# A ternary 3x3 convolution after group norm: work ahead of image 0 reordered, Newton step and edge rows on ScalarE

## The chip, the cores and the metric

The kernel runs on one core of a Trainium2 chip. The metric is device time in microseconds for one execution. The core has TensorE (PE: matmul, PEld: its weight loads), VectorE (DVE), ScalarE (ACT), GpSimd (POOL) and SyncE (SP, which only issues DMAs here).

## What is computed

The input x has 32 images of 128 channels and 56 x 56 pixels, float32. Each image is normed in 32 groups of 4 channels, convolved 3 x 3 with weights made ternary, and added to itself.

```python
def _quantize(weight, Wp, Wn):
    max_val = jnp.max(jnp.abs(weight))
    safe_max = jnp.where(max_val > 0, max_val, jnp.ones_like(max_val))
    w_norm = jnp.where(max_val > 0, weight / safe_max, weight)
    delta = THRESHOLD * jnp.max(jnp.abs(w_norm))
    tern = jnp.where(w_norm > delta, 1.0, jnp.where(w_norm < -delta, -1.0, 0.0)).astype(weight.dtype)
    wq = jnp.where(tern > 0, Wp[0] * tern, jnp.where(tern < 0, Wn[0] * tern, tern))
    return wq
wq = _quantize(weight, Wp, Wn)
out = jax.lax.conv_general_dilated(x, wq, window_strides=(1, 1), padding=((1, 1), (1, 1)), ...)
return out + bias[None, :, None, None]
def _gn(v, G=32, eps=1e-05):
    ...
    return ((g - m) / jnp.sqrt(s + eps)).reshape(v.shape)
x = x + _L0_conv_ref(_gn(x), L0_conv_weight, L0_conv_bias, L0_conv_Wp, L0_conv_Wn)
```

THRESHOLD is 0.05, and m and s are mean and variance of a group in one image. In the inputs Wp and Wn are both 1.

## The kernel before

**Planes.** Channels lie on the 128 partitions. The three kernel rows are replaced by four products on half as many rows: from the 28 even and 28 odd rows of an image VectorE makes plane C (even + odd - 2 mean, `make_c`), D (odd - even, `make_d`) and A (differences of neighbouring odd rows, `make_a`), and GpSimd makes B (differences of even rows, `difference_b`, once the low part of C of the same image is there). One row of A and one of B lie at the image's edge, and ScalarE fills them (`edges`). The arrays `plane[0..3]` are shared by all images, one after another.

**Parts.** Each plane is scaled by the image's `norm_scale` and split into two float16 parts: ScalarE writes the high part (`make_hi`), VectorE the low one (`make_lo`, which needs the high). TensorE multiplies per product 4 banks of 6 matmuls (`multiply`), C and A into the even rows' PSUM banks, D and B into the odd rows'. A accumulates upon C and B upon D, so ScalarE copies the finished C and D products out in between (`copy_c`, `copy_d`), and VectorE combines each pair into y (`output_rows`, four passes, `y e` and `y o`). GpSimd issues a DMA that adds x, and SP stores y.

**Statistics.** ScalarE sums an image (`sum_x`), TensorE averages over the group with a one-column matmul, ScalarE takes the mean (`take_mean`), sums squares (`sum_squares`), TensorE averages, and VectorE makes the negated variance (`variance`). Then ScalarE takes a square root (`root`), VectorE its reciprocal (`first_rstd`), and VectorE refines it with one Newton step in two instructions (`newton_factor`, `scale_of_x`), which gives `norm_scale`.

**Order.** Every engine's order is written by hand in its `emit(prev, now, nxt, far)`, one slot for each image `now`: products and outputs of `now`, planes and factor of `nxt`, sum and mean of `far`. Engines meet only by semaphores, and a waiting instruction holds up everything behind it on its engine. There are a slot ahead of image 0 (`first_slot`, only `nxt`), the slot of image 0 (`second_slot`), then the ordinary ones, of which 24 lie in a loop. In an ordinary slot VectorE does: low D, variance, low A, planes C and D of the next image, reciprocal, Newton, low B, plane A, low C, four outputs. ScalarE does: high A, high B, copy C, root, sum, copy D, high C, mean, high D, squares, edges.

**Ahead of image 0.** ScalarE's queue issues the DMAs for wp, wn, the weights and the bias, and SP's issues those of images 0 to 3 in halves. VectorE finds the largest weight, makes the ternary weights (`w_pos`), and TensorE turns and combines them into four sets (`turn_weights`), which VectorE casts (`turned_weights`). TensorE then does 11 matmuls on constants (`warm_up`). `half_hi_ready` and `half_lo_ready` let the first product start upon half a plane. A second pass over everything follows only if Wp and Wn differ, which they don't here.

## Time and profile before

| | us |
|---|---|
| median of 3 executions | 574.85 (574.74 to 574.89) |
| profiled execution | 575.64 |
| its span, first to last instruction | 574.0 |
| VectorE busy | 542.9 (95%) |
| TensorE busy | 534.1 (93%) |
| ScalarE busy | 504.4 (88%) |
| GpSimd busy | 166.2 (29%) |
| mean granted TensorE clock | 0.989 of full |

Busy shares are of the span. Matmuls overlap, so TensorE's share counts time with at least one in flight. Times below are us from the span's start. The clock 1.00 is 2.4 GHz and 0.50 is 1.2 GHz.

### The profile page before, as it was taken

Reading aid. Unit: us, or ns where it says so; the run is one execution under the profiler, and the core shown is the slowest. Engines: PE = TensorE matmul, PEld = TensorE weight load, DVE = VectorE, ACT = ScalarE, POOL = GpSimd, SP = SyncE. Lnnn points to the kernel's source line nnn. Section 1 sums busy time; section 2 is a strip of 40 time slices with the busy share of each in tenths; the row PEclk is TensorE's granted clock in tenths of the full one; section 3 lists DMA queues with packets and bytes.
Section 4 is the critical chain, followed back from the end, with each engine's and each line's share of the span. In section 5 each row is a group of like instructions: output and inputs, shape, how many; then the busy total and the mean of one; then the engine's idle time right before and its main releaser. Section 6 shows DMA issues by size and latency. Waiting matters only on the chain.

```text
span 574.0 us, 9367 instructions
## 1 busy us (share of the span) xinstructions
PE 534.1 (93%) x3238; PEld 320.1 (56%) x3238; DVE 542.9 (95%) x506; ACT 504.4 (88%) x485; POOL 166.2 (29%) x107
## 2 busy tenths in 40 slices
PE   0597999999999999999999999999999999999994
PEld 0453555555555555555555555565555555555552
DVE  1986999999999999999999999999999999999994
ACT  3588999999999999999999999999999999999850
POOL 2203312333332223333222333332233333212330
PEclk9997999999999999999999999999999999999998
DMA  8433999999999999999999999999999999998767
GB/s 297 192 113 87 257 280 271 301 288 248 316 263 299 311 297 259 314 302 286 273 272 293 294 288 293 303 294 272 288 310 274 286 295 308 274 282 200 160 181 271
DMA packets 28104, 153.43 MB, mean 267 GB/s; under 512 B 3504, under 2 KB 3504, under 8 KB 28080
## 3 DMA queue, kind: packets, MB, share of 16 engines
q1 hardware_dynamic: 18576, 102.77, 47.1%
q0 software_dynamic: 8928, 49.78, 44.9%
q10 hardware_dynamic: 576, 0.59, 0.3%
q8 instruction: 12, 0.20, 0.1%
q14 instruction: 12, 0.10, 0.0%
HBM read 101.75 MB, written 51.38 MB: 267 GB/s over the span
## 4 chain that ended last, share of the span: by engine, by line
DVE 68%; issue 24%; PE 4%; DMA 2%; DVEq 1%; ACT 1%; ACTq 0%
DVE parts L581 25%; DVE y L600 18%; DVE plane L541 10%; DVE plane L547 10%; DMA y<-in_L_conv_weight_dram 2%; PE even_rows L732 2%; DVE newton L570 2%; PE odd_rows L732 1%; DVEq L157 1%; DVE plane L553 1%; DVE neg_var L559 1%; ACT parts L386 1%; DVE rstd L565 0%; PE even_rows L697 0%; DVE parts L587 0%
## 5 line engine op out<-in xcount | busy, mean ns | idle before, releaser
L732 PE MATMUL odd_rows<-parts,w_lhsT 128*128 128x385 f16 (+1 forms) x1536 | 266.8, 330 | 8.6 <-DVE parts L581 7.5
L732 PE MATMUL even_rows<-parts,w_lhsT 128*128 128x385 f16 (+1 forms) x1536 | 267.6, 331 | 3.7 <-DVE parts L587 2.9
L581 DVE SCALAR_TENSOR_TENSOR parts<-plane,norm_scale,parts 128x1568 f16<-128x1568 f32 x127 | 233.4, 1842 | 4.3 <-ACT parts L386 4.3
L324 POOL TENSOR_TENSOR plane<-x 128x1512 f32<-128x1512 f32 x32 | 109.2, 3413 | 384.1 <-DVE parts L581 366.9
L732 PEld LDWEIGHTS even_rows<-parts,w_lhsT 128*128 128x128 f16 x1536 | 150.0, 98 | 111.9 <-issue 8.7
L732 PEld LDWEIGHTS odd_rows<-parts,w_lhsT 128*128 128x128 f16 x1536 | 148.1, 100 | 108.2 <-DVE parts L581 9.4
L386 ACT ACTIVATE parts<-plane,norm_scale 128x1568 f16<-128x1568 f32 x127 | 199.8, 1597 | 9.8 <-ACT plane L426 5.2
L432 ACT ACTIVATE junk<-x,negmean 128x3136 f16<-128x3136 f32 x32 | 92.9, 2904 | 0.0
L392 ACT ACTIVATE junk<-x 128x3136 f16<-128x3136 f32 x31 | 86.9, 2804 | 0.0
L600 DVE SCALAR_TENSOR_TENSOR y<-even_rows,out_scale,d_sb 128x784 f32<-128x784 f32 x62 | 61.0, 1025 | 0.0
L600 DVE SCALAR_TENSOR_TENSOR y<-odd_rows,out_scale,c_sb 128x784 f32<-128x784 f32 x62 | 60.9, 1023 | 0.0
L541 DVE SCALAR_TENSOR_TENSOR plane<-x,neg2mean 128x1568 f32<-128x1568 f32 x32 | 59.0, 1844 | 0.0
L547 DVE TENSOR_TENSOR plane<-x 128x1568 f32<-128x1568 f32 x32 | 57.4, 1794 | 0.0
L377 ACT ACTIVATE d_sb<-odd_rows,bias_sb,out_scale 128x1568 f32<-128x1568 f32 x32 | 52.6, 1645 | 5.3 <-PE odd_rows L732 5.3
L337 POOL DMA_DIRECT2D y<-in_x_dram x62 | 54.4, 891 | 3.1 <-DVE y L600 0.5
L553 DVE TENSOR_TENSOR plane<-x 128x1512 f32<-128x1512 f32 x32 | 55.2, 1726 | 0.0
L371 ACT ACTIVATE c_sb<-even_rows,bias_sb,out_scale 128x1568 f32<-128x1568 f32 x32 | 52.5, 1641 | 1.7 <-PE even_rows L732 1.7
L417 ACT ACTIVATE neg2mean<-odd_rows 128x1 f32<-128x1 f32 x32 | 5.4, 170 | 26.5 <-PE odd_rows L718 21.9
L688 PE MATMUL odd_rows<-ident,w_absmax 128*128 128x128 f32 x1 | 0.4, 446 | 14.1 <-DVE w_absmax L503 14.1
L718 PEld LDWEIGHTS odd_rows<-sums,group_mean 128*128 128x128 f32 x62 | 10.9, 190 | 4.1 <-issue 1.8
L723 PEld LDWEIGHTS odd_rows<-sums,group_mean 128*128 128x128 f32 x64 | 11.6, 195 | 2.8 <-DVE parts L581 0.8
L503 DVE TENSOR_REDUCE w_absmax<-y 128x1 f32<-128x1152 f32 x1 | 1.4, 1353 | 11.6 <-DMA y<-in_L_conv_weight_dram 11.6
(65 smaller groups left out, 127.2 us busy)
## 6 DMA issues: line engine op xcount, KB each, us to landing
x<-in_x_dram SPq DMA_DIRECT2D x64, 784.0 KB, 11.7
out_dram<-y SPq DMA_DIRECT2D x63, 784.0 KB, 5.7
y<-in_x_dram POOLq DMA_DIRECT2D x62, 784.0 KB, 11.8
out_dram<-y SPq DMA_DIRECT2D x2, 392.0 KB, 6.2
y<-in_L_conv_weight_dram ACTq DMA_DIRECT2D x1, 576.0 KB, 10.7
wp_sb<-in_L_conv_Wp_dram ACTq DMA_DIRECT2D x1, 0.5 KB, 6.3
wn_sb<-in_L_conv_Wn_dram ACTq DMA_DIRECT2D x1, 0.5 KB, 7.9
bias_sb<-in_L_conv_bias_dram ACTq DMA_DIRECT2D x1, 0.5 KB, 12.2
```

The lines of the kernel that those rows point to most:

```text
L324: nc.gpsimd.tensor_tensor(plane[B][:, 0:PAIRS - 1, :], even[:, 0:PAIRS - 1, :], even[:, 1:, :], ALU.subtract).then_inc(plane_ready[B], 1)
L337: pool.dma_start(y, of, accum_op=ALU.add).then_inc(residual_added[img.buf][h], 16)
L377: nc.scalar.activation(d_sb[:], product_ps(ODD), ACT.Identity, bias=(no_bias if p else bias_sb)[:, 0:1], scale=out_scale[:, p, 1:2]).then_ ...
L386: nc.scalar.activation(part(img, j, HI), plane[j][:], ACT.Copy, scale=norm_scale[:, b_slice(img)]).then_inc(hi_ready[j], 1)
L392: nc.scalar.activation(junk[:], x_sb[img.buf][:].rearrange("p h w -> p (h w)"), ACT.Copy, accum_out=sums[:, img.buf, 1:2]).then_inc(sum_re ...
L432: nc.scalar.activation(junk[:], x_sb[img.buf][:].rearrange("p h w -> p (h w)"), ACT.Square, bias=negmean[:, b_slice(img)], accum_out=sums[ ...
L541: nc.vector.scalar_tensor_tensor(plane[C][:], xs[:, 0:H:2, :], neg2mean[:, b_slice(img)], xs[:, 1:H:2, :], ALU.add, ALU.add).then_inc(plan ...
L547: nc.vector.tensor_tensor(plane[D][:], xs[:, 1:H:2, :], xs[:, 0:H:2, :], ALU.subtract).then_inc(plane_ready[D], 1)
L553: nc.vector.tensor_tensor(plane[A][:, 1:, :], odd[:, 1:, :], odd[:, 0:PAIRS - 1, :], ALU.subtract).then_inc(plane_ready[A], 1)
L581: nc.vector.scalar_tensor_tensor(part(img, j, LO), plane[j][:], norm_scale[:, b_slice(img)], part(img, j, HI), ALU.mult, ALU.subtract).the ...
L600: nc.vector.scalar_tensor_tensor(rows_of(y_sb[img.buf], h, odd), product_ps(odd, 2 * h, 2 * h + 2), out_scale[:, p, 0:1], other[:, 2 * h:2 ...
L732: ins = nc.tensor.matmul(product_ps(odd, b, b + 1)[:, 0, :, to:to + n], w_lhsT[:, prod, kw, :], part(img, prod, which)[:, b * BANK_ROWS:(b ...
```

## The change

It does four things.

1. **Newton step on ScalarE.** VectorE keeps the reciprocal. The rest, in two instructions there, becomes three on ScalarE (square, times negated variance plus 3, times the first value), each waiting for the one before. In an ordinary slot they stand after the sum and ahead of `copy_d`.
2. **Edge rows in one instruction.** The four planes become one array `planes`, so that both edge rows can be reached with one stride.
3. **Ahead of image 0.** The weights' DMA is first on ScalarE's queue; SP waits for it before it loads image 1. VectorE makes plane D between the largest weight and the ternary weights, and the output scales move to slot 0. TensorE sums the variance ahead of turning the weights, its warm-up has 6 matmuls, and the mean of image 1 follows it. ScalarE sums image 1 ahead of the first high parts. The turned A and B weights are cast after the first low parts, on which C no longer waits.
4. **Slots 0 and 1.** In slot 0 VectorE makes planes A and B of image 0, ScalarE takes mean and squares of image 1 first, and TensorE sums its variance between two banks of D. Plane A of image 1 moves from slot 0 to slot 1.

For a second pass the weights are loaded again.

```diff
-WARM_UP = 11
+WARM_UP = 6
...
-        plane = [sb(f"plane{j}", [P, PAIRS, W]) for j in range(4)]
+        planes = sb("planes", [P, 4, PAIRS, W])
+        plane = [planes[:, j] for j in range(4)]
...
@@ SP: emit
                             if img.buf != nxt.buf or img is nxt:
+                                if p == 0 and img is far:
+                                    sp.wait_ge(w_loaded, 16)
                                 load(img, 0, first=img is nxt)
...
@@ GpSimd: emit
-                    if nxt:
-                        difference_b(nxt, after_c=now)
+                    if now and nxt:
+                        difference_b(nxt)
...
@@ ScalarE
+            act.dma_start(w_raw, weight.rearrange("o i h w -> o (i h w)")).then_inc(w_loaded, 16)
             act.dma_start(wp_sb[:], wp.rearrange("(a b) -> a b", a=1).broadcast_to([P, 1])).then_inc(scalars_loaded, 16)
...
-                    xs, bias = x_sb[img.buf], negmean[:, b_slice(img)]
-                    nc.scalar.activation(plane[A][:, 0, :], xs[:, 1, :], ACT.Identity, bias=bias)
-                    nc.scalar.activation(plane[B][:, PAIRS - 1, :], xs[:, H - 2, :], ACT.Identity,
-                                         bias=bias).then_inc(edges_ready, 1)
+                    first, last = A * PAIRS, B * PAIRS + PAIRS - 1
+                    rows = planes[:].rearrange("p j r w -> p (j r) w")[:, first:last + 1:last - first, :]
+                    nc.scalar.activation(rows, x_sb[img.buf][:, 1:H - 1:H - 3, :], ACT.Identity,
+                                         bias=negmean[:, b_slice(img)]).then_inc(edges_ready, 1)
...
+                def scale_of_x(img):
+
+                    b = b_slice(img)
+                    act.wait_ge(rstd_ready, img.count(plus=1))
+                    nc.scalar.activation(rstd_sq[:, b], rstd0[:, b], ACT.Copy, scale=rstd0[:, b]).then_inc(rstd_sq_ready, 1)
+                    act.wait_ge(rstd_sq_ready, img.count(plus=1))
+                    nc.scalar.activation(newton[:, b], rstd_sq[:, b], ACT.Identity, bias=three[:, 0:1],
+                                         scale=neg_var[:, b]).then_inc(newton_ready, 1)
+                    act.wait_ge(newton_ready, img.count(plus=1))
+                    nc.scalar.activation(norm_scale[:, b], newton[:, b], ACT.Copy,
+                                         scale=rstd0[:, b]).then_inc(scale_of_x_ready, 1)
...
@@ VectorE
-                def newton_factor(img):
-                    b = b_slice(img)
-                    dve.wait_ge(rstd_ready, img.count(plus=1))
-                    nc.vector.tensor_scalar(newton[:, b], rstd0[:, b], rstd0[:, b], neg_var[:, b],
-                                            ALU.mult, ALU.mult).then_inc(newton_ready, 1)
...
+                def make_first_b(img):
+                    plane_free(img, B)
+                    even = x_sb[img.buf][:, 0:H:2, :]
+                    nc.vector.tensor_tensor(plane[B][:, 0:PAIRS - 1, :], even[:, 0:PAIRS - 1, :], even[:, 1:, :],
+                                            ALU.subtract).then_inc(plane_ready[B], 1)
...
@@ TensorE: emit
                         sum_first_mean(nxt)
-                        turn_weights()
                         pe.wait_ge(negmean_ready, nxt.count(plus=1))
                         sum_var(nxt, start=True)
+                        turn_weights()
                         warm_up()
+                        pe.wait_ge(var_ready, nxt.count(plus=1))
+                        sum_mean(far, start=True)
                     if second_slot:
-                        pe.wait_ge(w_ready, 4 * p + 4)
+                        pe.wait_ge(w_ready, 4 * p + 2)
```

How the orders stand now, at three places. First ScalarE in an ordinary slot, from the high parts of A and B to the means of the image after next. `parts` is the high part, `junk,sums<-x` the sum, `std` the root. Before:

```order
L386 ACTIVATE parts<-plane,norm_scale 128x1568 x2
L371 ACTIVATE c_sb<-even_rows,bias_sb,out_scale 128x1568
L438 ACTIVATE std<-neg_var 128x1
L392 ACTIVATE junk,sums<-x 128x3136
L377 ACTIVATE d_sb<-odd_rows,bias_sb,out_scale 128x1568
L386 ACTIVATE parts<-plane,norm_scale 128x1568
L417 ACTIVATE neg2mean<-odd_rows 128x1
```

and in the change:

```order
L392 ACTIVATE parts<-planes,norm_scale 128x1568 x2
L377 ACTIVATE c_sb<-even_rows,bias_sb,out_scale 128x1568
L444 ACTIVATE std<-neg_var 128x1
L398 ACTIVATE junk,sums<-x 128x3136
L451 ACTIVATE rstd_sq<-rstd 128x1
L453 ACTIVATE newton<-rstd_sq,three,neg_var 128x1
L456 ACTIVATE norm_scale<-newton,rstd 128x1
L383 ACTIVATE d_sb<-odd_rows,bias_sb,out_scale 128x1568
L392 ACTIVATE parts<-planes,norm_scale 128x1568
L423 ACTIVATE neg2mean<-odd_rows 128x1
```

The three Newton instructions have come in between the sum and the copy of D. The first waits for VectorE's reciprocal, and the copy of D and the high part of C stand behind them.

Second, VectorE in the same slot, from the low part of A to the low part of C of the next image (`parts` is the low part, `plane<-x` are planes C, D and A). Before:

```order
L581 SCALAR_TENSOR_TENSOR parts<-plane,norm_scale,parts 128x1568
L541 SCALAR_TENSOR_TENSOR plane<-x,neg2mean 128x1568
L547 TENSOR_TENSOR plane<-x 128x1568
L565 RECIPROCAL rstd<-std 128x1
L570 TENSOR_SCALAR newton<-rstd,neg_var 128x1
L576 TENSOR_SCALAR norm_scale<-newton,rstd 128x1
L581 SCALAR_TENSOR_TENSOR parts<-plane,norm_scale,parts 128x1568
L553 TENSOR_TENSOR plane<-x 128x1512
L581 SCALAR_TENSOR_TENSOR parts<-plane,norm_scale,parts 128x1568
```

In the change:

```order
L616 SCALAR_TENSOR_TENSOR parts<-planes,norm_scale,parts 128x1568
L582 SCALAR_TENSOR_TENSOR planes<-x,neg2mean 128x1568
L588 TENSOR_TENSOR planes<-x 128x1568
L612 RECIPROCAL rstd<-std 128x1
L616 SCALAR_TENSOR_TENSOR parts<-planes,norm_scale,parts 128x1568
L594 TENSOR_TENSOR planes<-x 128x1512
L616 SCALAR_TENSOR_TENSOR parts<-planes,norm_scale,parts 128x1568
```

The two Newton instructions behind the reciprocal are gone, and nothing else of this slot has moved on VectorE.

Third, VectorE ahead of image 0 and at the start of slot 0, from the ternary weights on. Before:

```order
L523 SCALAR_TENSOR_TENSOR w_pos<-y,w_consts,w_neg 128x1152
L541 SCALAR_TENSOR_TENSOR plane<-x,neg2mean 128x1568
L531 CAST w_lhsT<-even_rows 128x384 x2
L559 TENSOR_SCALAR neg_var<-odd_rows 128x1
L531 CAST w_lhsT<-even_rows 128x384
L565 RECIPROCAL rstd<-std 128x1
L570 TENSOR_SCALAR newton<-rstd,neg_var 128x1
L576 TENSOR_SCALAR norm_scale<-newton,rstd 128x1
L531 CAST w_lhsT<-odd_rows 128x384
L547 TENSOR_TENSOR plane<-x 128x1568
L587 SCALAR_TENSOR_TENSOR parts<-plane,norm_scale,parts 128x784 x2
L553 TENSOR_TENSOR plane<-x 128x1512
```

In the change:

```order
L551 SCALAR_TENSOR_TENSOR w_pos<-y,w_consts,w_neg 128x1152
L606 TENSOR_SCALAR neg_var<-odd_rows 128x1
L582 SCALAR_TENSOR_TENSOR planes<-x,neg2mean 128x1568
L612 RECIPROCAL rstd<-std 128x1
L572 CAST w_lhsT<-even_rows 128x384 x2
L622 SCALAR_TENSOR_TENSOR parts<-planes,norm_scale,parts 128x784 x2
L572 CAST w_lhsT<-odd_rows 128x384 x2
L616 SCALAR_TENSOR_TENSOR parts<-planes,norm_scale,parts 128x1568
L594 TENSOR_TENSOR planes<-x 128x1512
```

The variance has moved ahead of plane C, plane D to a place before the ternary weights (not in the piece), and the third and fourth casts of weights behind the two half passes of the low part.

## Rows read from the trace of the kernel before

**Rows 1.** The page's part 4, chain that ended last: share of the span by engine.
```profile
DVE 68%; issue 24%; PE 4%; DMA 2%; DVEq 1%; ACT 1%; ACTq 0%
```

**Rows 2.** Timeline, VectorE, one steady period: start us, duration us, engine, line, operation.
```profile
313.94 1.84 DVE L581 SCALAR_TENSOR_TENSOR parts<-plane,norm_scale,parts 128x1568 f16<-128x1568 f32 x1
...
326.53 0.16 DVE L565 RECIPROCAL rstd<-std 128x1 f32<-128x1 f32 x1
326.72 0.27 DVE L570 TENSOR_SCALAR newton<-rstd,neg_var 128x1 f32<-128x1 f32 x1
...
327.16 1.84 DVE L581 SCALAR_TENSOR_TENSOR parts<-plane,norm_scale,parts 128x1568 f16<-128x1568 f32 x1
...
330.56 1.84 DVE L581 SCALAR_TENSOR_TENSOR parts<-plane,norm_scale,parts 128x1568 f16<-128x1568 f32 x1
```

**Rows 3.** Timeline, ScalarE, the same period; in brackets idle time and releaser.
```profile
317.56 0.33 ACT L425 ACTIVATE plane<-x,negmean 128x56 f32<-128x56 f32 x1
317.80 0.33 ACT L426 ACTIVATE plane<-x,negmean 128x56 f32<-128x56 f32 x1
318.30 3.10 ACT L386 ACTIVATE parts<-plane,norm_scale 128x1568 f16<-128x1568 f32 x2 [0.17 <-ACT plane L426]
...
325.73 1.64 ACT L377 ACTIVATE d_sb<-odd_rows,bias_sb,out_scale 128x1568 f32<-128x1568 f32 x1
327.28 1.60 ACT L386 ACTIVATE parts<-plane,norm_scale 128x1568 f16<-128x1568 f32 x1
329.67 0.17 ACT L417 ACTIVATE neg2mean<-odd_rows 128x1 f32<-128x1 f32 x1 [0.80 <-PE odd_rows L718]
```

**Rows 4.** Groups by line and form, ScalarE: busy us, mean ns | idle before.
```profile
L371 ACT ACTIVATE c_sb<-even_rows,bias_sb,out_scale 128x1568 f32<-128x1568 f32 x32 | 52.5, 1641 | 1.7 <-PE even_rows L732 1.7
L425 ACT ACTIVATE plane<-x,negmean 128x56 f32<-128x56 f32 x32 | 10.6, 332 | 0.0
```

**Rows 5.** Timeline, ScalarE, mean and squares of image 0.
```profile
15.32 0.17 ACT L418 ACTIVATE negmean<-odd_rows 128x1 f32<-128x1 f32 x1
15.52 2.91 ACT L432 ACTIVATE junk<-x,negmean 128x3136 f16<-128x3136 f32 x1
```

**Rows 6.** Timeline, VectorE, first output passes of image 1 and of image 30.
```profile
66.47 1.97 DVE L600 SCALAR_TENSOR_TENSOR y<-even_rows,out_scale,d_sb 128x784 f32<-128x784 f32 x2
...
548.33 1.97 DVE L600 SCALAR_TENSOR_TENSOR y<-even_rows,out_scale,d_sb 128x784 f32<-128x784 f32 x2
```

**Rows 7.** The page's part 6, the weights' DMA: KB, us from issue to landing.
```profile
y<-in_L_conv_weight_dram ACTq DMA_DIRECT2D x1, 576.0 KB, 10.7
```

**Rows 8.** Timeline, all engines, ahead of and in slot 0.
```profile
7.20 1.51 ACT L400 ACTIVATE junk<-x 128x1568 f16<-128x1568 f32 x1 [2.39 <-DMA x<-in_x_dram]
...
9.07 1.51 ACT L403 ACTIVATE junk<-x 128x1568 f16<-128x1568 f32 x1 [0.27 <-ACT junk L400]
...
14.61 0.29 DVE L512 TENSOR_REDUCE w_max<-odd_rows 128x1 f32<-128x128 f32 x1 [0.27 <-PE odd_rows L688]
...
17.60 1.42 DVE L523 SCALAR_TENSOR_TENSOR w_pos<-y,w_consts,w_neg 128x1152 f16<-128x1152 f32 x1
...
25.91 1.97 DVE L587 SCALAR_TENSOR_TENSOR parts<-plane,norm_scale,parts 128x784 f16<-128x784 f32 x2
...
27.08 4.15 PE L732 MATMUL even_rows<-parts,w_lhsT 128*128 128x392 f16 x24 [2.88 <-DVE parts L587]
...
47.86 1.97 DVE L600 SCALAR_TENSOR_TENSOR y<-even_rows,out_scale,d_sb 128x784 f32<-128x784 f32 x2
```

**Rows 9.** Windows: us, busy of PE, PEld, DVE, ACT, POOL (count), PEclk, DMA, GB/s.
```profile
24.20:27.00 2.80, 0.00 (x0) 0.00 (x0) 2.80 (x3) 2.00 (x3) 0.14 (x1) 1.00 0.00 0
...
46.20:47.20 1.00, 0.98 (x4) 0.55 (x5) 1.00 (x1) 1.00 (x1) 0.00 (x0) 0.59 0.00 0
...
52.00:53.00 1.00, 1.00 (x5) 0.46 (x4) 1.00 (x1) 1.00 (x2) 1.00 (x2) 0.50 0.59 63
...
299.09:531.72 232.63, 229.24 (x1402) 137.88 (x1401) 231.62 (x212) 219.27 (x211) 72.19 (x42) 1.00 1.00 285
```

More of the change, by code:

```diff
@@ L788, in emit @@
                         pe.wait_ge(d_ready, now.count(plus=1))
[L789 to L791 removed]
+                        if far and not second_slot:
                             sum_mean(far, start=False)
```

170 lines of the change are left out of this document (93 added, 77 removed).

## Prediction

> **What bounds the kernel now.** I read the page's chain of waits first. It lies on VectorE for 68% of the span, and another 24% is "issue", time between instructions in which nothing is waited for [rows 1]. So I went to the timeline of VectorE in the middle of the run. From one low-part pass over plane C (313.94) to the next (330.56) there are 16.62 us, and VectorE starts each instruction as the one before runs out [rows 2]. The first output pass of image 1 starts at 66.47 and that of image 30 at 548.33, so 29 periods last 481.86 us, 16.616 us each [rows 6]. VectorE is the bound of every slot. ScalarE has one real gap in its slot, 0.80 us ahead of the mean, and a gap of 0.17 us where it waits for its own edge rows [rows 3]. It is nearly as full, and this is what matters here, since the change takes work from the fullest engine and gives it to the next.
>
> Ahead of image 0 it is different. Slot 0 starts its products at 27.08 and its outputs at 47.86 [rows 8]. From there to 66.47 are 18.61 us, 2.0 more than a period, with TensorE at half its clock between them [rows 9].
>
> **The steady slots, what goes.** VectorE loses the two Newton instructions. The reciprocal starts at 326.53 and the next large instruction at 327.16, 0.63 us later [rows 2]; with the reciprocal alone I take 0.09, an estimate: its 0.16 less an overlap of 0.07 with the next. VectorE's own work falls by 0.54 to 16.08 us. ScalarE's second edge instruction starts 0.24 after the first [rows 3] and goes; the one that stays has 56 more columns. Those are about 0.05 us, by 332 ns for 56 columns against 1.60 us for 1568 [rows 3, 4]. That is 0.19 less on ScalarE.
>
> **What comes.** ScalarE gets three dependent instructions of one column each between its sum pass and its copy of D, and they start only when VectorE's reciprocal has ended. I call the time from the start of the first to the start of the copy of D x. An instruction of 56 columns with one operand read per partition takes 332 ns, of which 47 are columns, leaving 285 ns [rows 4]. The second one reads two such operands. The copy of C, also with two, takes 1641 ns for 1568 columns where the high part with one takes 1600, and it reads PSUM, which the small mean pass at 0.17 us shows to be no slower [rows 3, 4]; I take 365 ns. Between an instruction and one that needs its result, ScalarE let 0.03 us pass: the negated mean ends at 15.49, the squares that read it start at 15.52 [rows 5]. After the last, the next independent instruction starts 0.09 before its end, as the second edge row starts at 317.80 while the first, begun at 317.56, lasts 0.33 [rows 3]. So x = 0.285 + 0.03 + 0.365 + 0.03 + 0.19 = 0.90 us. The low end takes the three as short as the mean pass with no such operand, 0.17: 0.17 + 0.03 + 0.17 + 0.03 + 0.08 = 0.48. The high end takes both gaps as 0.17, as at the edge rows, where three other waits stand at the same instruction [rows 3]: 1.18. I take 0.90, since the edge instruction is the nearest row in shape and operands and the mean's gap the nearest wait.
>
> The Trainium skill, page "ScalarE: Activation LUTs", section "What ACT_TABLE_LOAD costs", gives 186 ns plus 93 for each per-partition operand; by it the second instruction would be 372 ns and x 0.91, an estimate from that page beside my 0.90. The same page, "Rules for kernel authors", puts adds and multiplies on VectorE rather than ScalarE. Its reason is speed per element, which one column doesn't test; the rows say 0.54 us off one engine for 0.90 on the other.
>
> **Why the new place costs.** Follow the loop that the change closes. The low part of C starts on VectorE (313.94); with the four output passes, the low parts of D and A, planes C and D back to back, the reciprocal starts 12.59 us later (326.53) and lasts 0.16 [rows 2]. ScalarE sees it 0.03 later, the gap that VectorE's own next step leaves (326.69 to 326.72). Then x. Then the copy of D, which the order puts ahead of the high part of C, holds ScalarE 1.55 (325.73 to 327.28); the high part lasts 1.60 [rows 3]; 0.03 later the low part of C of the next image can start. The sum is 12.59 + 0.16 + 0.03 + x + 1.55 + 1.60 + 0.03 = 15.96 + x. No shift of one engine against another can shorten it, since it returns to where it began one image later. With x = 0.90 a period is 16.86 us. In the kernel before, the high part of C needed only VectorE's own factor, and the copy of D ran beside the Newton step; that loop had slack. Break-even is x = 16.616 - 15.96 = 0.66. Told on VectorE: it saves 0.54 at the reciprocal and then waits some 0.8 ahead of the low part of C. Over 29 periods this is 29 * (16.86 - 16.616) = **+7.1 us**. The ends of x give 29 * (-0.18) = -5.2 and 29 * 0.52 = +15.1.
>
> ScalarE alone can't bound the slot: its work was 16.62 - 0.89 us (the gap before the mean, from 328.78, 1.50 after the high part's start, to 329.67) = 15.73, less 0.19, plus x: 16.44. The copy of D comes later against TensorE's last product, by my sums with some 0.1 to 0.2 us to spare.
>
> **Ahead of image 0.** The weights are now the first DMA on their queue, and SP holds back images 1 to 3 until they land. Their landing took 10.7 us from their issue [rows 7]. Issued at about 1 us the bounds are 11.7 and, by the first half of image 0, which is larger and was being summed at 7.20, about 7 [rows 8]. I take 8.2, nearer to the low end, as only image 0 competes. The second half of image 0 was there at 9.07 [rows 8]; sharing with the weights I take 9.4. Then follow, with the durations that the same instructions had before, its sum (1.51 and 0.19 for the accumulator), the mean by way of TensorE (0.9, an estimate), squares (2.91 and as much around them as makes 3.2) and variance (0.6, an estimate): 9.4 + 1.7 + 0.9 + 3.2 + 0.6 = 15.8. VectorE in parallel: maximum at 8.2, plane D 9.5 to 11.2, the ternary chain 14.61 to 19.02 before (4.41), with its new step 4.6 [rows 8], so also 15.8. Then plane C and the reciprocal 17.8, x, and now the sum of image 1 (2.8) stands ahead of the first high half, which starts at 21.5. From the first low half to the first product it was 27.08 - 25.91 = 1.17 [rows 8], so products start at 23.6, **3.5 us earlier**. Slot 0 then: C to 27.6, D from 27.6; variance of image 1 after D's second bank; output scales after it at 30.9, on which the copy of C now waits; copies of C and D 31.1 and 34.2; Newton 35.8; high part of C of image 1 36.8; low part 38.4; outputs 40.2 instead of 47.86, **7.7 earlier**. Two things take some back. Plane A of image 1 is made only after the outputs (end 47.5), so the high part of A starts there; from a high part of A to the sum's end are 7.43 us (318.30 to 325.73) [rows 3], then x, 1.55, 1.60 and 1.77 for the low part of C (its 1.84 less the overlap): outputs of image 1 at 60.8 instead of 66.47. **-5.7 us** with TensorE at full clock.
>
> **TensorE's clock.** Between its warm-up (to 24.2) and 27.08 TensorE idled 2.9 us and the granted clock stayed 1.00, that is 2.4 GHz. After 3 us with little to do at the end of slot 0 it was 0.59 on average over 46.2 to 47.2 and 0.50 (1.2 GHz) up to 53, four microseconds into dense products that began at 49 [rows 9]. In the change the warm-up is 6 matmuls of 384 columns instead of 11 and ends near 20.0 (after 15.8, three microseconds of turned weights and 1.2 of its own); the first product is at 23.6, a gap of 3.6 us with one tiny matmul inside. That is longer than either, so I take half clock for the first 4 us of C: 2.0 us lost, of which 0.25 is covered by VectorE, that arrives at the variance only at 30.5. The start then gives -5.7 + 1.75 = **-3.95 us**.
>
> The Trainium skill, "TensorE: Matmul & The Clock Gate", "The HAM clock gate (the "warmup" mystery)", says that the monitor's windows run freely and the turning point varies between runs of one kernel. By that the two rivals at either clock could both occur; the rows here show one execution only.
>
> **The sum.** -3.95 + 7.1 = +3.1 us. The profiled execution took 575.64 with a span of 574.0; against its span the changed one is 577.1. The median shown is 574.85, and the difference carries over: **578.0 us**. The tail after image 31 keeps its order (no sum is left for it, and the last planes wait on GpSimd as before), so 0.
>
> **Rivals.**
> 1. TensorE stays at full clock at the start: -5.7 + 7.1 = +1.4, 576.3. For it: the gap of 2.9 us that cost nothing.
> 2. The self-waits are long: gaps of 0.11 to 0.17, x 1.06 to 1.18, periods 17.02 to 17.14, +11.7 to +15.1 less 3.95: 582.6 to 586.0. For it: the only self-wait in the loop shows 0.17. Against: it carries several waits.
> 3. The other sign: the small instructions are short. The loop closes without loss at x = 0.66, and the whole change breaks even at x = 0.66 + 3.95/29 = 0.79, only 0.11 under my value. At x = 0.48 it is -5.2 - 3.95: 565.7; at 0.66, 570.9. For it: the small ones without operands take 0.17. Against: all rows with one such operand show 0.285 beyond the columns.
> 4. The start doesn't do what it says: the weights land at 10 or later although first, VectorE's ternary chain slips by 1.8 us or more, and the start gives 2 instead of 4: 580.
> 5. Some slack that I miss makes the loop no bound and VectorE's 0.54 us come free, TensorE then bounding: it is busy 229.24 of 232.63 us in the steady stretch [rows 9], 16.37 of a period. 574.85 - 29 * 0.25 - 4 = 563.6.
>
> **How the numbers follow.** Chances: forecast 0.42, rival 1 0.15, rival 2 0.15, rival 3 0.13, rival 4 0.10, rival 5 0.05. For the range I leave out rival 5, the lower half of 3 and the upper part of 2: 570.5 to 583.5. A measurement of this kernel tells 0.2% (1.15 us) from nothing, so slower begins at 576.0: forecast, rivals 2 and 4 and over half of rival 1, less a reserve for the thin margin of 0.11 us in x, 0.62; same 0.18; faster 0.20.
>
> **What would show it.** Right: periods of 16.8 to 16.9 between output passes; VectorE idle 0.7 to 0.9 us before the low part of C, released by ScalarE's high part; ScalarE idle some 0.3 us before the first Newton instruction, released by VectorE's reciprocal; x between 0.85 and 0.95; outputs of image 0 near 40 to 42; a granted clock of 0.50 about 24 to 28. Wrong: no idle time before the low part of C, or a period under 16.6.

## The result and the profile after

The changed kernel takes 581.07 us (median, 580.20 to 581.63), the one before 574.81 in the same set: a ratio of 1.0108, interval 1.009 to 1.0125, so 6.3 us slower. The forecast was 578.0 and slower, with a range to 583.5. The profiled execution took 581.24 with a span of 579.3.

I read it in the order in which the prediction read the kernel before. The page's part 4, the chain that ended last by engine, answers [rows 1]:

```profile
DVE 41%; issue 33%; ACT 18%; PE 4%; DVEq 1%; DMA 1%; ACTq 0%
```

VectorE's share of the chain has gone from 68% to 41%, and ScalarE's from 1% to 18%. Neither engine alone bounds a slot; the chain runs through both. The timeline of ScalarE in one steady period answers [rows 3]; brackets hold idle time and its releaser:

```profile
310.69 0.29 ACT L451 ACTIVATE rstd_sq<-rstd 128x1 f32<-128x1 f32 x1 [0.32 <-DVE rstd L612]
311.02 0.39 ACT L453 ACTIVATE newton<-rstd_sq,three,neg_var 128x1 f32<-128x1 f32 x1
311.44 0.29 ACT L456 ACTIVATE norm_scale<-newton,rstd 128x1 f32<-128x1 f32 x1
311.64 1.64 ACT L383 ACTIVATE d_sb<-odd_rows,bias_sb,out_scale 128x1568 f32<-128x1568 f32 x1
313.18 1.59 ACT L392 ACTIVATE parts<-planes,norm_scale 128x1568 f16<-128x1568 f32 x1
```

x is 311.64 - 310.69 = 0.95 us. The copy of D then holds ScalarE 1.54 us, and only behind it comes the high part of C. VectorE in the same period, which answers [rows 2]:

```profile
310.50 0.16 DVE L612 RECIPROCAL rstd<-std 128x1 f32<-128x1 f32 x1
310.57 1.84 DVE L616 SCALAR_TENSOR_TENSOR parts<-planes,norm_scale,parts 128x1568 f16<-128x1568 f32 x1
312.32 1.73 DVE L594 TENSOR_TENSOR planes<-x 128x1512 f32<-128x1512 f32 x1
314.81 1.85 DVE L616 SCALAR_TENSOR_TENSOR parts<-planes,norm_scale,parts 128x1568 f16<-128x1568 f32 x1 [0.76 <-ACT parts L392]
```

The reciprocal is followed at once (0.07) by the low part of B: the 0.54 us are saved. Then VectorE idles 0.76 us ahead of the low part of C. The view of waits (total us, times, longest) says that this is so in every slot, and that ScalarE is in turn held at the reciprocal:

```profile
DVE parts L616 <- ACT parts L392: 25.1, 32, 1.7
ACT rstd_sq L451 <- DVE rstd L612: 14.1, 30, 3.1
```

Each engine waits for the other once per image. That is what a loop through two engines looks like. The first output passes of images 1 and 30, VectorE's timeline, answer [rows 6]:

```profile
63.08 1.97 DVE L631 SCALAR_TENSOR_TENSOR y<-even_rows,out_scale,d_sb 128x784 f32<-128x784 f32 x2
...
553.18 1.97 DVE L631 SCALAR_TENSOR_TENSOR y<-even_rows,out_scale,d_sb 128x784 f32<-128x784 f32 x2
```

29 periods last 490.10 us, 16.900 each, where it was 16.616. That is +8.2. The start gave 66.47 - 63.08 = -3.4. From image 30's outputs to the end of the span are 26.1 us against 25.7, +0.45; the last output pass starts 17.91 us after image 30's first one in both kernels, so this lies behind the last pass, where only the last stores of y are left. Over all the kernels below this tail runs from 24.4 to 26.5 us; its cause stays open. The sum is +5.3, the difference of the two spans (579.3 and 574.0). The medians differ by 0.9 us more, since the profiled execution of before lay 0.8 above its median and that of after 0.2.

The start, ScalarE's timeline, which answers [rows 8]:

```profile
18.77 0.30 ACT L451 ACTIVATE rstd_sq<-rstd 128x1 f32<-128x1 f32 x1 [1.64 <-DVE rstd L612]
...
19.72 2.80 ACT L398 ACTIVATE junk<-x 128x3136 f16<-128x3136 f32 x1
...
22.52 1.77 ACT L417 ACTIVATE parts<-planes,norm_scale 128x784 f16<-128x784 f32 x2
...
33.12 1.66 ACT L377 ACTIVATE c_sb<-even_rows,bias_sb,out_scale 128x1568 f32<-128x1568 f32 x1 [1.64 <-DVE out_scale L564]
```

and TensorE's, with the end of its preparation and the first product. The PEld rows are the weight loads of the first product, one for each matmul:

```profile
19.08 2.13 PE L743 MATMUL odd_rows<-turn 128*128 128x384 f16 x6
...
22.75 0.35 PE L755 MATMUL odd_rows<-sums,group_mean 128*128 128x1 f32 x2 [1.55 <-ACT junk L398]
...
24.63 0.89 PEld L769 LDWEIGHTS even_rows<-parts,w_lhsT 128*128 128x128 f16 x6 [1.61 <-issue]
24.66 5.83 PE L769 MATMUL even_rows<-parts,w_lhsT 128*128 128x392 f16 x24 [1.55 <-DVE parts L622]
...
25.70 0.15 PEld L769 LDWEIGHTS even_rows<-parts,w_lhsT 128*128 128x128 f16 x1 [0.18 <-issue]
...
26.03 0.15 PEld L769 LDWEIGHTS even_rows<-parts,w_lhsT 128*128 128x128 f16 x1 [0.18 <-issue]
```

The first product starts at 24.66 instead of 27.08, but lasts 5.83 us instead of 4.15. The windows answer [rows 9]; the granted clock is the third number from the end:

```profile
24.00:26.00 2.00, 1.34 (x6) 0.71 (x7) 2.00 (x4) 1.97 (x5) 0.00 (x0) 0.81 0.00 0
26.00:27.00 1.00, 1.00 (x4) 0.44 (x3) 1.00 (x2) 1.00 (x1) 0.00 (x0) 0.50 0.00 0
27.00:28.00 1.00, 1.00 (x5) 0.45 (x4) 1.00 (x1) 1.00 (x1) 0.00 (x0) 0.50 0.00 0
...
29.00:30.00 1.00, 1.00 (x8) 0.59 (x7) 1.00 (x2) 0.12 (x1) 0.00 (x0) 1.00 0.00 0
```

The first product begins at 2.4 GHz (six weight loads in 0.89 us), falls to 1.2 GHz within its first microsecond (the next ones are 0.33 us apart), and is back at 2.4 GHz in the window from 29. It costs 1.7 us. The weights, the page's part 6, against [rows 7]:

```profile
y<-in_L_conv_weight_dram ACTq DMA_DIRECT2D x1, 576.0 KB, 6.9
```

### The profile page after: what moved, and what is told of

Read it like the earlier page. It is cut to its first block, busy times and chain, and to the rows that moved or that the text cites. A ratio compares the mean times of both kernels' runs of the same rounds, so it can differ in the third digit from the quotient of the medians.

```text
span 579.3 us, 9358 instructions
## 1 busy us (share of the span) xinstructions
PE 540.7 (93%) x3233; PEld 318.1 (55%) x3233; DVE 530.6 (92%) x443; ACT 525.4 (91%) x549; POOL 163.0 (28%) x106
## 4 chain that ended last, share of the span: by engine, by line
DVE 41%; issue 33%; ACT 18%; PE 4%; DVEq 1%; DMA 1%; ACTq 0%
DVE y L631 17%; DVE parts L616 10%; DVE planes L588 9%; ACT parts L392 9%; DVE planes L582 3%; ACT d_sb L383 2%; ACT newton L453 2%; PE odd_rows L769 2%; PE even_rows L769 2%; ACT rstd_sq L451 2%; DMA x<-in_x_dram 1%; ACT junk L398 1%; DVEq L161 1%; DVE neg_var L606 1%; ACT junk L438 1%
## 5 line engine op out<-in xcount | busy, mean ns | idle before, releaser
L616 DVE SCALAR_TENSOR_TENSOR parts<-planes,norm_scale,parts 128x1568 f16<-128x1568 f32 x127 | 233.4, 1843 | 25.1 <-ACT parts L392 25.1
L330 POOL TENSOR_TENSOR planes<-x 128x1512 f32<-128x1512 f32 x31 | 106.1, 3422 | 392.4 <-DVE parts L616 392.4
L392 ACT ACTIVATE parts<-planes,norm_scale 128x1568 f16<-128x1568 f32 x127 | 199.8, 1596 | 9.4 <-ACT planes L432 5.2
L582 DVE SCALAR_TENSOR_TENSOR planes<-x,neg2mean 128x1568 f32<-128x1568 f32 x32 | 59.1, 1848 | 0.0
L588 DVE TENSOR_TENSOR planes<-x 128x1568 f32<-128x1568 f32 x32 | 57.2, 1787 | 0.8 <-ACT junk L406 0.8
L594 DVE TENSOR_TENSOR planes<-x 128x1512 f32<-128x1512 f32 x32 | 55.4, 1730 | 0.0
L451 ACT ACTIVATE rstd_sq<-rstd 128x1 f32<-128x1 f32 x32 | 9.4, 295 | 14.1 <-DVE rstd L612 14.1
L755 PEld LDWEIGHTS odd_rows<-sums,group_mean 128*128 128x128 f32 x62 | 9.2, 188 | 16.6 <-issue 14.9
L755 PE MATMUL odd_rows<-sums,group_mean 128*128 128x1 f32 x62 | 11.6, 256 | 4.8 <-ACT junk L398 2.8
L760 PEld LDWEIGHTS odd_rows<-sums,group_mean 128*128 128x128 f32 x64 | 11.6, 194 | 5.6 <-issue 3.5
L453 ACT ACTIVATE newton<-rstd_sq,three,neg_var 128x1 f32<-128x1 f32 x32 | 12.4, 387 | 1.1
```

What stands on the lines that cost most here:

```text
L330: nc.gpsimd.tensor_tensor(plane[B][:, 0:PAIRS - 1, :], even[:, 0:PAIRS - 1, :], even[:, 1:, :], ALU.subtract).then_inc(plane_ready[B], 1)
L392: nc.scalar.activation(part(img, j, HI), plane[j][:], ACT.Copy, scale=norm_scale[:, b_slice(img)]).then_inc(hi_ready[j], 1)
L582: nc.vector.scalar_tensor_tensor(plane[C][:], xs[:, 0:H:2, :], neg2mean[:, b_slice(img)], xs[:, 1:H:2, :], ALU.add, ALU.add).then_inc(plan ...
L588: nc.vector.tensor_tensor(plane[D][:], xs[:, 1:H:2, :], xs[:, 0:H:2, :], ALU.subtract).then_inc(plane_ready[D], 1)
L594: nc.vector.tensor_tensor(plane[A][:, 1:, :], odd[:, 1:, :], odd[:, 0:PAIRS - 1, :], ALU.subtract).then_inc(plane_ready[A], 1)
L616: nc.vector.scalar_tensor_tensor(part(img, j, LO), plane[j][:], norm_scale[:, b_slice(img)], part(img, j, HI), ALU.mult, ALU.subtract).the ...
```

## The experiments

The theory: a loop of reciprocal, x, copy of D, high part of C and low part of C sets the period, since the copy of D stands behind the Newton step. The first rival: ScalarE is simply too full (**occupancy**), and any work on it costs the same wherever it stands. The second: the reordering or the joined edge rows cost the period, not the Newton step. Periods below are means over images 1 to 30, from the first output pass of each. Each ratio is to the kernel before in the same set of runs; periods and start times are those of one profiled execution of each kernel.

| kernel | edit | median us | ratio to before, 95% | period us | outputs of image 0, 1 |
|---|---|---|---|---|---|
| before | | 574.8 to 575.6 | 1 | 16.616 | 47.86, 66.47 |
| changed | | 581.07 | 1.0108 (1.009, 1.0125) | 16.900 | 42.28, 63.08 |
| e1 | changed, Newton on VectorE | 567.27 | 0.9857 (0.984, 0.9874) | 16.64 | 38.16, 58.16 |
| e2 | changed, copy of D first | 570.97 | 0.9926 (0.9909, 0.9942) | 16.577 | 41.80, 62.75 |
| e3 | before, Newton on ScalarE | 584.70 | 1.016 (1.0143, 1.0177) | 16.893 | 49.23, 68.50 |
| e4 | changed, 20 warm-up matmuls | 579.09 | 1.0067 (1.005, 1.0084) | 16.892 | 40.53, 61.33 |
| e5 | changed, pad inside the loop | 587.68 | 1.0213 (1.0196, 1.023) | 17.152 | 42.46, 63.52 |
| e6 | changed, pad outside it | 579.62 | 1.0072 (1.0056, 1.0089) | 16.895 | 42.51, 63.30 |
| e7 | before, joined edge rows | 575.65 | 1.0008 (0.9996, 1.0019) | 16.616 | 47.91, 66.91 |
| e8 | changed, Newton on GpSimd | 634.52 | 1.1039 (1.1018, 1.106) | 18.671 | 40.43, 63.61 |
| e9 | changed, sum of image 1 first | 578.17 | 1.0044 (1.0033, 1.0055) | 16.893 | 41.18, 61.97 |
| e10 | e1, Newton split between engines | 563.16 | 0.9784 (0.9764, 0.9805) | 16.468 | 38.27, 58.69 |
| e11 | e10, plane A of image 1 in slot 0 | 561.15 | 0.9752 (0.9736, 0.9768) | 16.460 | 41.77, 59.77 |
| e12 | e11, 10 warm-up matmuls | 560.26 | 0.9746 (0.973, 0.9763) | 16.460 | 39.57, 56.30 |

### One part alone: Newton back on VectorE, and Newton alone on ScalarE

```diff
@@ e1, VectorE: emit, all three slots
 first_rstd(nxt)
+newton_factor(nxt)
+scale_of_x(nxt)
@@ e1, ScalarE: emit, all three slots
-scale_of_x(nxt)
```

> The changed kernel with the Newton step back on VectorE, two instructions behind each reciprocal; the new start and the joined edge rows stay. Loop theory (the period is the closed loop low C, outputs, low D and A, planes C and D, reciprocal, Newton on ScalarE, copy of D, high C): without Newton and the copy of D in that loop VectorE's own 16.62 us bound again, so 29 x (16.62 - 16.90) = -8.2 us against the changed kernel, about 572.5 us, 2 to 3.5 under the kernel before, which is what the new start is worth. Rival (the joined edge rows or the one array of planes slow the steady slots): the period stays above 16.8 and the time above 579.

e3 makes the opposite edit in the kernel before: the two instructions leave VectorE, the three come on ScalarE ahead of `copy_d`, and nothing else is touched.

> The kernel before with only the Newton step moved to ScalarE, in ordinary slots between the sum and the copy of D; start, warm-up and edge rows as before. Loop theory: period 16.90, 29 x 0.28 = +8.2 us, about 583. Rival (the slowdown comes from something at the start or from the edge rows): 575 to 577.

e1 has the old period but for one longer slot at the start (17.30 after image 1), e3 has the new one. So the period belongs to the Newton step alone. In e3 VectorE idles 0.75 us ahead of the low part of C, as in the changed kernel. Its time is 1.7 us over the 583 expected: I had priced only the periods, and the step also makes the start 2.0 us longer (outputs of image 1 at 68.50 instead of 66.47).

e1 came out some 5 us better than I had written down, and nearly all of it lies ahead of image 1's outputs: 58.16 against 63.08. ScalarE's timeline in e1:

```profile
16.77 2.80 ACT L398 ACTIVATE junk<-x 128x3136 f16<-128x3136 f32 x1
...
19.57 1.77 ACT L417 ACTIVATE parts<-planes,norm_scale 128x784 f16<-128x784 f32 x2
```

Without the Newton step on its queue ScalarE sums image 1 at 16.77, while VectorE makes plane C and the reciprocal. In the changed kernel the sum stands behind the wait for the reciprocal (19.72), and the first high half and the first product come 2.95 us later. Of the other 2.0 us 1.7 are TensorE's clock, which stayed up in e1 (below).

So the whole change falls into two pieces. All of it but the Newton move is worth about -8 us (e1, 567.27 against 575.32). The Newton move takes back 13.8. By the spans of the profiled executions it is 13.4: 7.5 in the periods, 4.9 at the start, 1.0 behind image 30's first output pass.

### The order alone: the copy of D first

```diff
+copy_d(now)
 if nxt:
     scale_of_x(nxt)
-copy_d(now)
-if nxt:
     make_hi(nxt, C)
```

> The changed kernel with one line moved: in ordinary slots ScalarE does the copy of D before the Newton step instead of after it. The instructions and their number are the same. Loop theory: the copy of D (1.54 us) leaves the closed loop, which falls to 15.5 us; ScalarE's whole work then bounds, 16.90 less its wait of 0.33 for the reciprocal, plus 0.12 because the high part of C now follows the last Newton instruction directly, 16.69: -6 us against the changed kernel, about 575. Rival (ScalarE simply has too much to do, the order is beside the point): no more than 0.1 us per period, 578 to 581.

The same instructions on the same engines, two of them exchanged in the ordinary slots, give 0.32 us per period, more than the whole loss: 570.97 us. ScalarE's timeline in e2:

```profile
305.69 1.64 ACT L383 ACTIVATE d_sb<-odd_rows,bias_sb,out_scale 128x1568 f32<-128x1568 f32 x1
307.23 0.29 ACT L451 ACTIVATE rstd_sq<-rstd 128x1 f32<-128x1 f32 x1
...
308.30 1.60 ACT L392 ACTIVATE parts<-planes,norm_scale 128x1568 f16<-128x1568 f32 x1
```

There is no wait for the reciprocal any more, since it ends during the copy of D. ScalarE now runs without a gap but for 0.17 at the edge rows, and it is the bound: ordinary slots take 16.59 us, and one short one at the end (16.06) brings the mean to 16.58. I had put the period at 16.69. From the last row of the sum to the instruction behind it are 0.09 us, where there were 0.50: 0.41 less, and not only the 0.32 that the profile calls idle, since an instruction without a wait starts before the one ahead has run out. The high part of C costs 0.13 more, as it now waits for the last Newton instruction. The net is 0.28 of the 0.31.

### The same extra work inside and outside the loop

A copy of 200 columns to a tile that nobody reads, extra work only, is put on ScalarE in two places.

```diff
@@ e5
 scale_of_x(nxt)
+nc.scalar.activation(pad[:], no_bias[:].broadcast_to([P, 200]), ACT.Copy)
 copy_d(now)
@@ e6
 sum_squares(far)
+nc.scalar.activation(pad[:], no_bias[:].broadcast_to([P, 200]), ACT.Copy)
 edges(nxt)
```

> The changed kernel with one extra ScalarE instruction per ordinary slot (a copy of 200 columns from a constant, about 0.26 us of its time) between the Newton step and the copy of D, inside the closed loop. Nothing waits for it. Loop theory: the period grows by all of it, 16.90 to 17.16, +7.5 to +8 us over 30 slots, about 589. Occupancy theory (ScalarE's total work bounds): the same here; the next run tells them apart.

> The same extra instruction, the same number of times, but between the squares and the edge rows, outside the closed loop. Loop theory: ScalarE has 0.33 us of waiting for the reciprocal in each slot, which takes up the 0.26; the period stays 16.90 and the time within 1 us of the changed kernel, 581 to 582. Occupancy theory: as with the extra instruction inside, +7.5 us, 589.

ScalarE's timeline in e5:

```profile
315.60 0.35 ACT L494 ACTIVATE pad<-no_bias 128x200 f32<-128x200 f32 x1
315.86 1.64 ACT L384 ACTIVATE d_sb<-odd_rows,bias_sb,out_scale 128x1568 f32<-128x1568 f32 x1
```

The pad moves the copy of D by 0.26 us, and the period grows by 0.25, from 16.90 to 17.15. In e6 the same pad starts at 319.31 and the edge rows at 319.57, again 0.26, and the period is 16.895. ScalarE is as full in one as in the other: 533.1 us busy in both. The occupancy theory falls with this pair; the loop stands. (e6's median is 1.5 us under the changed kernel's, in another set; its period is the same, and I read nothing into it.)

### The edge rows alone

> The kernel before with only the edge rows joined into one instruction. VectorE bounds the slot, so ScalarE's 0.19 us saved per slot are not seen: 574.8, within 0.3. Rival (the four planes in one array, or the strided write, cost something): over 576.

The edit is the change's own, in the kernel before: `planes` as one array and both rows in one `activation`. The period is 16.616, and the interval of the ratio includes 1. The median, 575.65, is over the range that I gave and under the rival's. ScalarE loses 0.19 us per slot that it didn't need, as VectorE is the bound there. With e1 and e3 the second rival falls too.

### TensorE's clock at the first product

```diff
-WARM_UP = 6
+WARM_UP = 20
```

> The changed kernel with 20 warm-up matmuls instead of 6, which fill TensorE's idle time ahead of the first product. If the half clock over some 3.4 us of the first products is what slot 0 lost, its products gain 1.6 us and the time falls to 579.5, with the granted clock 1.00 from the first product on. Rival (slot 0 is bound by ScalarE and VectorE, TensorE's clock is hidden): within 0.4 us of the changed kernel, 581. The period stays 16.90 either way.

e4 gains 2.0 us and its first product takes 4.15 us, as expected. Its warm-up begins at the same half rate as that of the changed kernel and comes up to full rate during its seventh matmul, and then TensorE idles only 1.0 us ahead of the product.

What the clock did at the first product differs from kernel to kernel. The granted clock's column reads 1.00 in every window until the first change that it shows, even where matmuls run at half rate, so I go by the starts of matmuls: those of the warm-up, 384 columns each, are 0.32 us apart at 1.2 GHz and 0.16 at 2.4 GHz, and those of the product 0.33 and 0.165. That gives three cases:

| clock at the first product | kernel, and idle time of TensorE between warm-up and product, us | C product of image 0, us |
|---|---|---|
| was up and stayed up | before 2.88, e3 1.87, e10 1.15, e4 1.03, e1 0.72, e8 0.59, e12 0 | 4.15 |
| was up and fell, ahead of the product or within its first microsecond | changed 3.10, e2 3.10, e7 2.50 | 5.83, 5.83, 5.61 |
| had not come up yet | e6 2.90, e5 2.89, e9 1.63, e11 0.55 | 6.26, 6.29, 7.03, 5.95 |

The changed kernel is of the second kind. Its six warm-up matmuls all run at half rate (2.13 us, starts 0.32 apart), and the clock came up behind them: the one-column pair after 1.55 us of idle time takes 0.35 us there, and 0.56 after the same idle time in e5, where the clock had not come up. Then it fell, after TensorE had done nothing but that pair from 21.2 to 24.66. So the reading of the idle time fits these rows, though no run changes the idle time alone. Where the clock was up, idle time of 1.87 us or less cost nothing in six executions, and of the four with 2.50 us or more three lost the clock; before, at 2.88, kept it. e7 is the counterpart of before: the same instructions up to the product but for the joined edge rows, 11 warm-up matmuls that end at full rate (2.54 us in all), 0.38 us less of idle time, and a product that runs at half rate from its first matmul to 30.1 us.

```profile
22.09 2.54 PE L707 MATMUL odd_rows<-turn 128*128 128x384 f16 x11
27.13 5.61 PE L733 MATMUL even_rows<-parts,w_lhsT 128*128 128x392 f16 x24 [2.50 <-DVE parts L588]
```

More warm-up matmuls do two things: they let the clock come up, and they shorten the idle time. e4 does both at once and doesn't part them.

The Trainium skill, "TensorE: Matmul & The Clock Gate", section "The HAM clock gate (the "warmup" mystery)", says that the start is throttled, that activity releases the throttle, and that one kernel's turning point differs between runs. The runs agree: e10 and e11 have the same instructions up to the first product, at times up to 0.5 us apart, and one had the clock and the other didn't.

### The sum of image 1 ahead of the wait

```diff
@@ ScalarE: emit, first_slot
 root(nxt)
-scale_of_x(nxt)
 sum_x(far)
+scale_of_x(nxt)
 make_first_hi(nxt)
```

> The changed kernel with one line moved ahead of image 0: ScalarE sums image 1 before the Newton step instead of after it. In the changed kernel the sum began only at 19.72, behind the wait for VectorE's reciprocal; now it fills the time in which VectorE makes plane C. The first high half comes at 20.6 instead of 22.5. If the order of these two is what cost the start, the outputs of image 1 come at least 1.9 us earlier than 63.08, and up to 4 where TensorE's clock doesn't fall in a shorter gap; period 16.90 unchanged; 577 to 579. Rival (the 4.9 us that the kernel with the Newton step on VectorE gained at the start come from the Newton instructions' own length): under 1 us, over 580.

The sum now fills the wait of 1.64 us, and the first product starts at 22.35 instead of 24.66, 2.3 earlier. It then takes 7.03 us instead of 5.83, for in this execution the clock had not come up at all: the product runs at half rate from its first matmul to 28.2. Of the 2.3 us image 1's outputs keep 1.1 in the profiled execution, less than the 1.9 that I had asked for; by the ratios it is 0.6%, and the median of 578.17 is within the 577 to 579 expected, with single executions from 575.9 to 579.0. So the place of the sum costs something, but not all that e1 got back is its own: part of that was the clock.

### The Newton step on GpSimd

The idlest engine takes all of it, as four two-operand instructions of one column each.

```diff
@@ GpSimd: emit
+if nxt:
+    newton_step(nxt)   # square, * neg_var, + three, * rstd0
 if now and nxt:
     difference_b(nxt)
```

> The changed kernel with the Newton step on GpSimd, as four dependent one-column instructions ahead of plane B. VectorE is rid of it (16.08 us of own work) and ScalarE too. What GpSimd takes for it is not known: it may take up to about 1.6 us from the reciprocal on before the high part of C is late for VectorE. Within that the period falls to 16.2 to 16.4, where TensorE's matmuls bound: 29 x (16.3 - 16.90) = -17, about 563 to 566. Rival (each GpSimd instruction costs 0.5 us or more): the low part of C waits again, period 16.6 or more, 572 and up.

634.52 us, by far the worst. Timeline of VectorE, GpSimd and ScalarE in e8:

```profile
298.55 1.83 DVE L615 SCALAR_TENSOR_TENSOR parts<-planes,norm_scale,parts 128x1568 f16<-128x1568 f32 x1
298.72 3.36 POOL L350 TENSOR_TENSOR rstd_sq<-rstd 128x1 f32<-128x1 f32 x1 [5.63 <-DVE rstd L611]
300.30 1.72 DVE L593 TENSOR_TENSOR planes<-x 128x1512 f32<-128x1512 f32 x1
302.16 0.19 POOL L352 TENSOR_TENSOR newton<-rstd_sq,neg_var 128x1 f32<-128x1 f32 x1
...
302.92 1.60 ACT L407 ACTIVATE parts<-planes,norm_scale 128x1568 f16<-128x1568 f32 x1 [3.05 <-POOL norm_scale L356]
```

The first one-column product takes 3.36 us, the next ones 0.19 each. The profile's spans on GpSimd are rough, but the next product starts only at 302.16, and it needs this one. It starts 0.17 us into VectorE's low part of B and ends when VectorE's plane A has ended (302.02). x in the loop, here from the first product to the high part of C, is 4.20 us. The copy of D runs beside it, so the loop is 12.59 to the reciprocal's start, 0.24, 4.20 and 1.64 to the low part of C: 18.67, the period. The rival occurred, and by more than it said.

The Trainium skill, "SBUF — State Buffer", section "Who interferes with whom", says that a VectorE instruction with two inputs in SBUF contends with a GpSimd instruction that reads SBUF. The same page's section "Summary: rules for kernel authors" says that the second of the two to issue is fully blocked until the first finishes. Both passes of VectorE here are of that kind, and the row agrees; that GpSimd didn't get in between the two passes is in the row and not on the page.

### A version that uses what was found

e10 goes back to e1 and splits the step: VectorE makes the factor, one instruction; ScalarE makes 3 rstd and the final multiply-add, two instructions, only the last of which needs VectorE's factor. Both stand behind the copy of D.

```diff
@@ VectorE: emit, ordinary slots
 first_rstd(nxt)
 newton_factor(nxt)
-scale_of_x(nxt)
@@ ScalarE: emit, ordinary slots
 copy_d(now)
 if nxt:
+    final_scale(nxt)
     make_hi(nxt, C)
```

> A candidate built on the kernel with the Newton step on VectorE. In ordinary slots the step is split: VectorE makes the factor right behind the reciprocal (one instruction), ScalarE makes three times the reciprocal beside it and then the scale in one instruction, both after the copy of D. VectorE's own work is 16.62 less about 0.24, ScalarE's about 16.0, the closed loop under 15.5. Loop theory: VectorE bounds at 16.38, 29 x (16.38 - 16.64) = -7.5 against that kernel, about 560. Rival (TensorE or a wait not seen so far bounds above that): 16.5 or more, 564 or more.

```diff
@@ e11, VectorE: slot 0
 make_d(nxt)
+make_a(nxt)
 make_lo(nxt, C)
@@ e11, VectorE: ordinary slots
-if third_slot:
-    make_a(now)
```

> The same, with plane A of image 1 made in slot 0, ahead of the low part of C of image 1, instead of in slot 1 behind the outputs. In slot 1 ScalarE then no longer waits 2.2 us for that plane. Expected 1.7 us less than the split kernel, about 558; if slot 0 gets longer by the 1.64 us of the plane and slot 1 shorter by as much, no change.

e12 is e11 with `WARM_UP = 10`.

> The run with Newton split and plane A of image 1 made in slot 0, with 10 instead of 6 warm-up matmuls. Theory (the first C products ran at half clock because TensorE had idled before them): four more matmuls, 0.3 us each at half clock, fill the time up to the first low half, so the C product of image 0 takes 4.15 instead of 5.95 us, outputs of image 1 start up to 1.7 us sooner (near 58.1 instead of 59.77), periods unchanged at 16.46, and the time is 559.4 to 560. Rival (four more don't hold the clock up; what counts is when the dense work began): C still takes 5.8 or more, the time stays at 561.1 within 0.6.

e10 has a period of 16.468, where I had put 16.38. It alternates between 16.37 and 16.55, and two rows from the timeline of one kind of slot and one from the other show the reason:

```profile
309.57 1.84 DVE L623 SCALAR_TENSOR_TENSOR parts<-planes,norm_scale,parts 128x1568 f16<-128x1568 f32 x1
311.47 4.16 PE L781 MATMUL odd_rows<-parts,w_lhsT 128*128 128x392 f16 x24 [0.18 <-DVE parts L623]
...
327.56 0.28 PE L772 MATMUL odd_rows<-sums,group_mean 128*128 128x1 f32 x2
...
327.88 0.16 DVE L601 TENSOR_SCALAR neg_var<-odd_rows 128x1 f32<-128x1 f32 x1
```

VectorE and TensorE are now nearly level. In one slot TensorE waits 0.18 us for the low part of D; in the next it is behind, and VectorE waits as long for its variance sum (the low part of D started at 325.94 there, so it was free at 327.70). The chain of waits of e10 lies on TensorE for 46% and on VectorE for 39%. By this reading there is little left to win by moving VectorE's work. The median, 563.16, lies between the 560 expected and the rival's 564.

e11 is 2.0 us below e10 in the medians, with overlapping intervals, and 3 us above the 558 expected. Slot 1 shrinks from 20.42 to 18.00 us. The outputs of image 0 come 3.5 us later, 1.8 by the longer first product (5.95 us at the clock that had not come up, against 4.15) and the rest by the plane A. The profiled execution of e11, 563.91, is its slowest by 2.7 us; the others have no trace.

The reason that I gave for e12 doesn't hold: in e11 the clock had not come up before the product, whatever the idle time. e12's first product takes 4.15 us and starts without idle time, its outputs of image 1 start at 56.30, earlier than the 58.1 expected, and its slot 1 is 16.73 us, with a granted clock of 1.00 all through, where e11 had 0.50 from 43.5 to 46.0. But the medians are only 0.9 apart, in different sets, with overlapping intervals, so the last step isn't shown by the times. e11 and e12 both beat either kernel, e12 by 2.5% against before.

## Why the prediction was right, point by point

- **The bound before and the engine that pays.** Right. The change moved work off the bound engine and became slower.
- **x = 0.90.** Measured 0.95: 0.29, 0.39 and 0.20 to the copy of D, with gaps of 0.04 and 0.03. The groups' means are 295 and 387 ns, where the estimates from the edge row and the copy of C were 285 and 365. The second operand was under-sized: the two long instructions that I named differ by 41 ns, the sum has 80 without saying where from, and it costs 92 here. With 41 the forecast of the period would have been 16.82; that 0.90 came so near is partly luck. By the Trainium skill's page "ScalarE: Activation LUTs", section "What ACT_TABLE_LOAD costs", it is 93 ns, and the rows agree.
- **The loop 15.96 + x.** 16.90 - 0.95 = 15.95. Right to 0.01 us. VectorE's idle time (0.76) and ScalarE's (0.32) are within what the text named as its test. The steady term was +7.1 and came out at +8.2: 29 times 0.05 from x, less 0.01 per period from the rest of the loop.
- **ScalarE can't bound: 16.44.** In the changed kernel ScalarE's own work is 16.90 less the 0.41 that it loses at the reciprocal, 16.49; the term was 0.05 too small, by x. e2 shows ScalarE as the bound, at 16.59 in its order, where the high part of C costs 0.13 more. It didn't decide here. The joined edge rows save 0.18 (edge rows to high part of A: 0.56 after, 0.74 before), where the sum had 0.19.
- **The weights at 8.2.** VectorE's first step starts at 7.88. The second half of image 0 came 0.6 later than I took (its sum starts at 10.01). The first high half was put at 21.5 and came at 22.52, the first product at 23.6 and came at 24.66. Rival 4 didn't occur: the weights were early, and the start still gave 3.4 of its 3.95. The variance was ready at 16.9 instead of 15.8, 0.6 of it by this half, and that delay is what the first high half and the first product show.
- **The cost of the Newton move at the start.** The chain of the text had the sum of image 1 in the right place and at its price: reciprocal 17.8, x, 2.8 of the sum, 21.5. What it didn't say is that the sum stands behind the wait for the reciprocal only because the Newton step does, so that this wait is a part of the move to ScalarE. e1 puts the move's whole cost there at 4.9 us, the clock included. The total was right without this split, but a reader who wanted to keep the good part of the change would have looked only at the steady slots.
- **The clock at the first product, 2.0 us.** Right in kind and nearly in size (1.7): the clock was up, and it fell after the idle time. It fell some 0.6 us into the product (the granted clock is 0.76 on average over 25.0 to 25.5) and not ahead of it, and the half clock lasted 3.4 us, not 4. In part this is luck: in e9, e5, e6 and e11, with the same warm-up, the clock had not come up at all, a case that the text didn't have. Rival 1 rested on before's gap of 2.9 us that cost nothing; e7 lost the clock in a gap of 2.50 us with the same warm-up, so a gap of this size can go either way, and one execution of before couldn't tell.
- **Rival 2, gaps of 0.17.** Didn't occur: the self-waits are 0.03 and 0.04. The 0.17 ahead of the high part of A is there after the change too, where one edge instruction precedes it.
- **Rival 3, short instructions, and 5, no loop.** Both fell. x is 0.29 over the loop's break-even.
- **The tail, 0.** +0.45, not explained. The other part of the 3.1 us between forecast and result is that the profiled execution of before was 0.8 above its median, that of the changed kernel 0.2: +1.1 period, +0.55 start, +0.45 tail, +0.9 profiled execution against median, with 0.1 of rounding.

## What to carry to other kernels

Before you move a small instruction from the fullest engine to another, walk the loop: from the place where the result is used, around through every instruction that the other engine's order puts between, back to the same place one iteration later. If that sum is over the period, the move loses, whatever the busy shares say; and what matters first is what stands between the moved step and its consumer (e2 won 10 us by exchanging two calls). Only then count how much work each engine has.

## What the runs showed of the hardware that I had not expected

- The page's granted clock can read 1.00 while matmuls run at half rate, up to the first change that it shows: in e9 it reads 1.00 from 22.35 to 28.00 us, where 18 matmuls of 392 columns take 5.65 us. The distance between starts of matmuls or of their weight loads tells the truth.
- A TensorE at full clock lost it in three executions out of four in which it did next to nothing for 2.5 us or more ahead of the first product, and in none of six with 1.9 us or less.
- A GpSimd instruction on 128 x 1 elements took 3.36 us beside two VectorE passes and 0.19 alone.
